# A twelve-layer latent transformer on one core: the row of score maxima made from 16-bit operands in two attention layers, and the post-processing of each head pair placed elsewhere in TensorE's order in a third

## The reference, cut to what matters

```python
scores = jnp.einsum('bhqd,bhkd->bhqk', Q, K) / scale        # layer 1; then masked
attention = jax.nn.softmax(scores, axis=-1)
out = jnp.einsum('bhqk,bhkd->bhqd', attention, V)...reshape(...) @ W_proj.T + b_proj

attn = jnp.einsum('bhqd,bhkd->bhqk', l2norm(q) * s, l2norm(k)) + attn_bias   # layer 3
out = jnp.einsum('bhqk,bhkd->bhqd', jax.nn.softmax(attn, axis=-1), v) @ Wo + bo
```

```python
kv = jnp.concatenate([layer_norm(x), layer_norm(latents)], axis=1) @ Wkv
weight = softmax(mask(q @ k))        # per head
out = (weight @ v) @ Wout
```

## Time and profile before

| what | us |
|---|---|
| median of 3 executions | 2721.6 |
| lowest and highest | 2712.99 and 2723.27 |
| the profiled execution | 2712.99 |
| its span, first to last instruction | 2711.1 |
| of it, layer 1's loop | from 409 to 800 |
| of it, layer 2's units | from 1028 to 1657 |
| of it, layer 3's loop | from 2014 to 2465 |

### The profile page before, as it was taken

The page is one execution under the profiler, slowest core; times in us unless marked ns, Lnnn a source line. Parts: engine busy times, 40 slices in busy tenths (PEclk is TensorE's granted clock), DMA queues, the critical chain, the costliest instruction groups (busy, mean ns, idle before and its releaser), DMA issues. The chain is left out here.

```text
span 2711.1 us, 44601 instructions
## 1 busy us (share of the span) xinstructions
PE 2381.5 (88%) x17529; PEld 1502.4 (55%) x17529; DVE 1694.4 (62%) x3275; ACT 1173.3 (43%) x1945; POOL 888.9 (33%) x537
## 2 busy tenths in 40 slices
PE   7866779999988879999999998289889999998798
PEld 4734546666654445555565555155546666665555
DVE  4986355455448477888888853755565455544577
ACT  2326134444444115555555552344445555553344
POOL 5510042232206112222222200058653444333286
PEclk8987889999989979999999999699999999999999
DMA  3200453323213036576777552023323223220132
GB/s 112 63 1 4 129 154 82 88 67 105 65 42 116 20 96 132 119 143 118 141 144 138 103 106 61 0 84 103 105 61 79 63 65 77 62 61 21 48 94 67
DMA packets 358321, 226.30 MB, mean 83 GB/s; under 512 B 289769, under 2 KB 326338, under 8 KB 358114
## 3 DMA queue, kind: packets, MB, share of 16 engines
q1 hardware_dynamic: 355042, 215.07, 32.8%
q0 software_dynamic: 3072, 8.39, 1.1%
HBM read 114.74 MB, written 0.52 MB: 43 GB/s over the span
## 5 line engine op out<-in xcount | busy, mean ns | idle before, releaser
L98 PE MATMUL PS<-hot 128*128 128x512 f16 x529 | 162.6, 451 | 141.8 <-DVE l2a_t L2354 48.3
L3752 PE MATMUL PS<-l2x_rows,l2x_pth 128*128 128x512 f16 x832 | 200.3, 379 | 17.7 <-DVE l2x_mean L3947 17.7
L3665 POOL TENSOR_TENSOR l2x_rows<-l2x_rows,l2x_one 128x1024 f16<-128x1024 f32 (+1 forms) x32 | 61.6, 1930 | 418.3 <-DVE l2x_rows L1405 418.3
L3297 ACT ACTIVATE l3x_pT<-PS 128x512 f32<-128x512 f32 (+1 forms) x208 | 121.9, 592 | 147.8 <-PE PS L3137 145.4
L3426 DVE CUSTOM_DVE_ANT_0 l1x_junk<-PS,l1x_bias 128x1024 bf16<-128x1024 f32 (+1 forms) x128 | 123.3, 991 | 98.3 <-PE PS L3091 97.4
L98 PEld LDWEIGHTS PS<-hot 128*128 128x128 f16 x529 | 54.5, 112 | 230.2 <-issue 53.7
L3940 DVE TENSOR_TENSOR l2x_pl<-l2x_sc,l2x_ph 128x1664 f16<-128x1664 f32 x64 | 152.3, 2380 | 40.5 <-ACT l2x_ph L3821 37.8
L3426 DVE CUSTOM_DVE_ANT_0 l3x_junk<-PS,l3x_bias 128x1024 bf16<-128x1024 f32 (+1 forms) x128 | 123.6, 991 | 44.8 <-PE PS L3091 43.6
L3925 DVE CUSTOM_DVE_ANT_0 l2x_sc<-PS,l2x_bias 128x1665 f32<-128x1665 f32 x64 | 120.9, 1889 | 37.8 <-issue 36.9
L3839 ACT ACTIVATE l2x_meanT<-PS 128x256 f32<-128x256 f32 x64 | 24.5, 383 | 270.6 <-PE PS L3729 270.6
L3721 PE MATMUL PS<-l2x_kh,l2x_qth 128*128 128x512 f16 (+1 forms) x512 | 132.8, 341 | 3.8 <-DMA l2x_kl<-l2x_rows 3.8
(11 more groups left out here) (841 smaller groups left out, 6254.3 us busy)
## 6 DMA issues: line engine op xcount, KB each, us to landing
l2f_unit<-in_L_ffn_units_dram SPq DMA_DIRECT2D x36, 384.0 KB, 3.1
l3f_unit<-in_L_ffn_units_dram SPq DMA_DIRECT2D x34, 384.0 KB, 3.0
l1x_kst<-l1x_kh SPq DMA_DIRECT2D x128, 100.1 KB, 2.2
l3x_kst<-l3x_kh SPq DMA_DIRECT2D x128, 100.1 KB, 2.2
l2x_rows<-in_ctx_dram SPq DMA_DIRECT2D x8, 1536.0 KB
l1x_ctx<-in_ctx_t_dram SPq DMA_DIRECT2D x7, 1601.0 KB, 7.4
l3x_ctx<-in_ctx_t_dram SPq DMA_DIRECT2D x7, 1601.0 KB, 6.9
l1x_kst<-l1x_kl SPq DMA_DIRECT2D x64, 100.1 KB, 2.2
```

Source lines behind the costliest of these rows:

```text
L98: self.nc.tensor.matmul(self.PS[:, bank, :], self.hot[:, 0:P], self.hot[:], start=True, stop=True)
L3297: nc.scalar.activation(to, of, ACT.Exp, scale=1.0 / S_SCALE).then_inc(exp_done, 1)
L3665: nc.gpsimd.tensor_tensor(high, of, one[0:p, 0:n].unsqueeze(2).unsqueeze(3).to_broadcast([p, n, NC, P]), ALU.mult).then_inc(rows_high, 1)
L3752: nc.tensor.matmul(PS[:, ACC, :], pth[:, u % 2, m, :], rows2[:, b % 2, :, :, m, :], start=(m == 0), stop=False)
```

## The change

It has two parts that do not meet. In `context_attention` the column of maxima is scaled by -1 / 2^15 and stored as f16 (`minus`) by a new DVE operation behind L3432, and M multiplies it with an f16 identity (`ident16`) instead of fp32 by fp32; ACT's copy no longer scales. POOL makes `ident16` with one more operation in the opening, and the `hot_made` semaphore counts that operation alone. In `layer_2_xattn`, `turn_means(u-1)` moves from inside the high matmuls to a place right behind `scores(u+2)`, ahead of the fills, and `project(u-1)` moves from the second low matmul to the eighth high one.

```diff
+        ident16 = sb("ident16", [P, P], F16)
+        minus = sb("minus", [P, R], F16)
...
-                for i, half in enumerate((slice(0, S), slice(S, P)) if normed else (slice(0, P),)):
+                for half in ((slice(0, S), slice(S, P)) if normed else (slice(0, P),)):
...
-                    nc.gpsimd.tensor_scalar(one_hot[half]..., ONE_HOT, None, ALU.mult).then_inc(hot_made, 1)
-                    pool.wait_ge(hot_made, i + 1)
+                    link(nc.gpsimd.tensor_scalar(one_hot[half]..., ONE_HOT, None, ALU.mult))
+                nc.gpsimd.tensor_copy(ident16[:], k.ident[:]).then_inc(hot_made, 1)
...
-                        pe.wait_ge(hot_made, 2 if normed else 1)
+                        pe.wait_ge(hot_made, 1)
...
-                            last = nc.tensor.matmul(PS[3 * F:3 * F + 1, bank, i * P:(i + 1) * P], both[:, u:u + 1],
-                                                    k.ident[:], start=True, stop=True)
+                            last = nc.tensor.matmul(PS[3 * F:3 * F + 1, bank, i * P:(i + 1) * P], minus[:, u:u + 1],
+                                                    ident16[:], start=True, stop=True)
...
-                                             ACT.Copy, scale=-1.0 / M_SCALE).then_inc(row_made, 1)
+                                             ACT.Copy).then_inc(row_made, 1)
...
-                            v.tensor_reduce(both[:, us], rmax[:, us, :], AX.X, ALU.max).then_inc(max_made, 1)
+                            link(v.tensor_reduce(both[:, us], rmax[:, us, :], AX.X, ALU.max))
+                            v.tensor_scalar(minus[:, us], both[:, us], -1.0 / M_SCALE, None, ALU.mult).then_inc(max_made, 1)
...
-    MEANS_AT, VALUES_AT = 4, 1
+    VALUES_AT = 7
...
                     if u + 2 < U:
                         scores(u + 2)
+                    if u > 0:
+                        turn_means(u - 1)
                     for group, of in fills(b, r):
                         prepare(group, of)
                     pe.wait_ge(high_turned, 16 * (u + 1))
                     pe.wait_ge(sums_copied, u)
                     for m in range(KT):
-                        if u > 0 and m == MEANS_AT:
-                            turn_means(u - 1)
+                        if u > 0 and m == VALUES_AT:
+                            project(u - 1)
                         nc.tensor.matmul(PS[:, ACC, :], pth[:, u % 2, m, :], rows2[:, b % 2, :, :, m, :], start=(m == 0), stop=False)
                     pe.wait_ge(low_turned, 16 * (u + 1))
                     for m in range(KT):
-                        if u > 0 and m == VALUES_AT:
-                            project(u - 1)
                         last = nc.tensor.matmul(PS[:, ACC, 0:D], ptl[:, u % 2, m, :], rows2[:, b % 2, 0, :, m, :], start=False,
```

More of the change, by code:

```diff
@@ L2961, in _ @@
                 split_weights(1, "v")
-                for i, half in enumerate((slice(0, S), slice(S, P)) if normed else (slice(0, P),)):
+                for half in ((slice(0, S), slice(S, P)) if normed else (slice(0, P),)):
                     of = k.ident[half, half if normed else slice(0, S)]
-                    nc.gpsimd.tensor_scalar(one_hot[half].rearrange("p (i s) -> p i s", s=S),
-                                            of.unsqueeze(1).to_broadcast([of.shape[0], BANK // S, S]), ONE_HOT, None,
-                                            ALU.mult).then_inc(hot_made, 1)
-                    pool.wait_ge(hot_made, i + 1)
+                    link(nc.gpsimd.tensor_scalar(one_hot[half].rearrange("p (i s) -> p i s", s=S),
+                                                 of.unsqueeze(1).to_broadcast([of.shape[0], BANK // S, S]), ONE_HOT, None, ALU.mult))
+                nc.gpsimd.tensor_copy(ident16[:], k.ident[:]).then_inc(hot_made, 1)
                 def hold():
```

## The result

| | before | after |
|---|---|---|
| median of 5 executions, us | 2722.86 | 2747.99 |
| lowest and highest | 2712.99, 2723.27 | 2738.17, 2749.89 |
| profiled execution, and its span | 2712.99, 2711.1 | 2720.26, 2718.5 |

The ratio is 1.009, with a 95% interval of 1.0063 to 1.0116: the change costs 25 us. The forecast was 2713.6, in a range of 2704 to 2724.

The account below looks back on a forecast made before the run. PE was taken to bound the loops of all three layers. M's 13.7 us less and layer 2's 5.7 more gave -8.0, so 2705.0 from the profiled 2713.0, or 2713.6 scaled to the median; range 2704 to 2724.

Parts of the forecast that it names:

- the cost of the new operation: DVE's added operation ahead of M in layers 1 and 3: 0.19 us with its link, bounds 0.10 and 0.30.
- step 25 of layer 3: PE's wait ahead of M grows from 0.66 to 0.85 us; net gain 0.40 each, 7 times, 2.8 us.
- M's passes: M in layers 1 and 3, four f16 passes for eight fp32: PE free 0.59 us earlier each; M's sum 13.7 less.
- step 18 of layer 1: Behind M, A[11] waits for ACT's tick and starts 0.34 us earlier; 14 such places at steps 18 or 20, 4.8 us.
- Step 25 of layer 1: New operation hidden ahead of M, gain 0.59 each, 7 times, 4.1 us; a wait appearing there would prove the forecast wrong.
- Layer 2: Reordered means and project: no PE passes gained, waits moved; sum 5.7 us more, bounds 0 and 14.
- wait ahead of the fills in r = 2: Six layer 2 units: transposes wait for late means with fills behind them, 0.81 us each, 4.9 us more.
- exposed weight loads: Layer 2 transposes in their new place: fp32 loads stick out about 0.05 us in 38 units, 1.9 us more (0 to 3).
- units of r = 3: Layer 2: no stall expected for the means; if it stays, 0.6 us more in each of 12 units (with r = 6).
- Reorder free: Rival: layer 2's earlier exponential pulls the means forward, so nothing stalls in r = 2; near 2707 us, chance 0.18.
- Every wait in layer 2 is paid: Rival: the transposes' two waits cost 0.20 + 0.08 us in 63 units; net +15, 2736 us, chance 0.10.
- PE has headroom: Rival: ACT's row or next exponential ends the waits at every M, half of 13.7 comes back; 2720 us, chance 0.15.

Follow-up runs that it names:

- e3_op_alone: The kernel before with only the new VectorE tensor_scalar added, its result read by nothing: ratio 1.0097, 26 us slower.
- e4_reduce_f16: The change's M part without the new operation (the reduction writes f16, ScalarE's copy keeps the scale), layer 2 as before: ratio 0.9944, 15 us faster than before.
- e2_order_alone: The kernel before with only the change's layer 2 reorder: ratio 1.0001 (0.9986 to 1.0016).
- e5_reduce_f16_order: The M part with the f16 reduction instead of the new operation, plus the change's layer 2 order: ratio 0.9968, 9 us faster than before.
- e11_reduce_f16_again: Repeat on another occasion of the M part with the f16 reduction and no new operation, layer 2 as before: ratio 0.9956, 12 us faster than before.
- e10_all_pieces: The change's M part alone, with GpSimd's two context operations and the weight split L2387 each cut into four: ratio 0.9984, 4 us faster than before.

## Why the prediction was wrong

**The step that failed** is the cost of the new operation: "Its nearest row is L3927, 0.15 us; with the link ahead of it I take 0.19", in layer 1 "hidden, with 0.2 to spare", in layer 3 "Bounds for the DVE operation are 0.10 and 0.30". The size is right for 9 of 16 in layer 1 and 12 of 16 in layer 3, and where it is right its price is too: six of the seven waits at step 25 of layer 3 are 0.86 to 0.87 us, and 0.85 was forecast. The bounds were wrong, since they took an operation's duration for a property of the operation: 0.17 alone, 5.77 to 6.15 beside a GpSimd operation that had begun 0.5 to 1.8 us before, up to 6.96 in the experiments. The forecast looked at GpSimd for what the change adds to it (nothing) and never asked what runs on it while the new operation does. e3_op_alone shows the operation alone to be worth 26 us; e4_reduce_f16 shows the change's M part without it to be worth -15.

**The trace of before had it all.** It has a `tensor_scalar` of the very form of the new operation, 128x4 from SBUF, ahead of layer 2's units. L3989 takes 1.60 us and ends at 973.89, 0.03 behind the end of the GpSimd operation (L3665 lasts until 973.86):

```profile
971.97 1.89 POOL L3665 TENSOR_TENSOR l2x_rows<-l2x_rows,l2x_one 128x1024 f16<-128x1024 f32 x1
972.29 1.60 DVE L3989 TENSOR_SCALAR l2x_norm_var<-l2x_norm_mean_var 128x4 f32<-128x4 f32 x1
```

The row that the forecast took as the nearest, L3927, could not have warned: it is a `tensor_scalar` too, with one element in each partition instead of four, and it takes 0.15 us in all 64 units, also where GpSimd is in the middle of an operation. What lets it through no run here tests.

```profile
1063.85 2.13 POOL L3670 TENSOR_TENSOR l2x_rows<-l2x_rows 128x1024 f16<-128x1024 f32 x1
1064.79 0.15 DVE L3927 TENSOR_SCALAR l2x_shift<-l2x_rmax 128x1 f32<-128x1 f32 x1
```

In layer 2, L3940, an operation with both inputs in SBUF, has the tile row 1873/1893/3616 ns, and all 21 of its 64 that are over 2.2 us start where a GpSimd operation began just before:

```profile
1109.11 1.89 POOL L3665 TENSOR_TENSOR l2x_rows<-l2x_rows,l2x_one 128x1024 f16<-128x1024 f32 x1 [35.84 <-DVE l2x_rows L1405]
1109.14 3.62 DVE L3940 TENSOR_TENSOR l2x_pl<-l2x_sc,l2x_ph 128x1664 f16<-128x1664 f32 x1
1111.08 3.66 POOL L3670 TENSOR_TENSOR l2x_rows<-l2x_rows 128x1024 f16<-128x1024 f32 x1
```

3.62 is 1.86 to the end of L3665 (1111.00) and 1.76 of work, near its usual 1.89. And the places where the new operation would start were to be read, too; this is step 20 of a batch of layer 3:

```profile
2179.14 6.27 POOL L3013 TENSOR_TENSOR l3x_ctxl<-l3x_ctx,l3x_ctxh 128x3202 f16<-128x3202 f32 x1
2179.45 0.16 DVE L3432 TENSOR_REDUCE l3x_both<-l3x_rmax 128x4 f32<-128x8 f32 x1
```

The new operation would be ready at 2179.66 and could start at 2185.41, 5.75 later. It was measured at 5.77. The other long ones can be had in the same way: a second batch has the same pattern (2300.30 to 2306.06), L2387 runs from 2429.24 to 2437.20 with the last L3432 at 2431.32, and in six batches of layer 1 L3013 ends 0.4 us behind the end of L3432 at step 25. Some 17 us of holding in layer 3's loop stood in rows that I had not set side by side.

**M's passes** were right. L3100 is four f16 passes, 0.38 to 0.59 us long as merged rows, and e4_reduce_f16 has layer 1's attention 6.9 us shorter (forecast 2.4 + 4.1 + 1.0 = 7.5) and layer 3's 6.8 and 7.4 (forecast 6.2 with the operation, 7.7 by the same terms without it). At step 18 of layer 1, from M to A[11], 1.60 us stand where 1.95 stood (730.93 to 732.53), 0.35 against the forecast 0.34, and A[11] waits for ACT's tick as said:

```profile
730.93 0.38 PE L3100 MATMUL PS<-l1x_ident,l1x_minus 128*1 128x128 f16 x4
...
732.53 0.42 PE L3092 MATMUL PS<-l1x_kst,l1x_qst 96*128 96x512 f16 x2 [0.24 <-ACT l1x_act_tick L3267]
```

Step 25 of layer 1 in the change: a wait of 0.33 appeared, the very row that the forecast named as its refutation.

**Layer 2** was right in mechanism and about right in size: forecast +5.7, measured +4.2 in after, +3.7 and +3.9 in e2_order_alone and e5_reduce_f16_order. The wait ahead of the fills in r = 2 is there (0.60 in five of the six units, 0.72 in unit 26), and against e4_reduce_f16 the high matmuls of these units start 0.77 us later behind those of the unit before (0.90 in unit 26), where the forecast had 0.81. The make-up is only partly the forecast's. The exposed weight loads (1.9) didn't come: in unit 31 of the earlier trace rows, the transposes start right behind the scores without idle and the high matmuls behind them:

```profile
1318.54 0.22 PE L3723 MATMUL PS<-l2x_kh,l2x_qtl 128*128 128x129 f16 x1
1318.59 0.39 PE L3731 MATMUL PS<-ident,l2x_mean 128*128 128x128 f32 x2
...
1318.82 1.67 PE L3756 MATMUL PS<-l2x_rows,l2x_pth 128*128 128x512 f16 x7
```

Three units of r = 3 have a wait for the means, as unit 27 (1.02 us), but such waits aren't new: before has two (units 11 and 43) and e4_reduce_f16 three, and against e4_reduce_f16 these units lose only 0.1 to 0.3 us. The last units ran at a granted clock of 0.76 (1618 to 1632) where before had 1.00 (1638 to 1652), and from unit 62 to unit 63 took 8.95 us against 6.24. That can't be put down to the order alone: e11_reduce_f16_again has the old one and takes 7.92 there.

**The rivals.** "Reorder free" fell to the traces (+4), though the whole time can't tell it from no change. "Every wait in layer 2 is paid" had the sign of the result and nearly its size (+15 against 25), and was wrong in place: e2_order_alone is at 1.0001. "PE has headroom" fell: the freed passes came out as shorter loops in e4_reduce_f16. The case that happened, an operation on VectorE held by GpSimd, was not among them.

## What to carry to other kernels

A VectorE operation has two prices: its own, and what is left of the GpSimd operation that it starts beside, if its form is one that waits; where GpSimd operations follow each other without a break, it can be several of them (6.76 us in the section below). Before adding one, read GpSimd's rows at each place where it would start, and look in the tile rows of VectorE for a maximum far from the median. Where the operation must be on a critical list, let an operation that isn't held write the wanted type itself, and put the factor where it costs nothing: here the reduction wrote f16, ScalarE's copy kept the scale, and a loss of 25 us became a gain of 12 to 15.

## What the runs showed of the hardware

Beside the same kind of GpSimd operation (6.25 us, SBUF to SBUF), a 128x4 `tensor_scalar` from SBUF took 5.77 us, a `tensor_tensor` with two inputs in SBUF 5.98 us, and a `tensor_reduce` 0.16 us. A 128x1 `tensor_scalar` took 0.15 us beside one. GpSimd can be the one held too: L3670 above took 3.66 us, until 2.0 us after L3940 ended.

A held operation doesn't always get in when the first GpSimd operation ends. In before, L3989 and the two `tensor_scalar` behind it each got in at the end of one L3665, though the next followed without a break. But the operation behind them, a 128x4 `scalar_tensor_tensor` with both inputs in SBUF, was held past one L3665 and three L3670, until 984.38:

```profile
977.52 0.60 POOL L3665 TENSOR_TENSOR l2x_rows<-l2x_rows,l2x_one 64x256 f16<-64x256 f32 x1
977.62 6.76 DVE L123 SCALAR_TENSOR_TENSOR l2x_norm_tmp<-l2x_norm_rstd 128x4 f32<-128x4 f32 x1
978.09 6.89 POOL L3670 TENSOR_TENSOR l2x_rows<-l2x_rows 128x1024 f16<-128x1024 f32 x4
```

In e10_all_pieces, where the pieces wait for one another in between, the `tensor_scalar` beside L2387 got through in 0.83 us. Pieces without these waits were not tried.

TensorE idle for 5.16 us in a loop otherwise at 2.4 GHz was followed by 10 us at a mean granted clock of 0.67, and the stall cost 7.7 us in all against e4_reduce_f16.
